# Mixing weights computed in place, a new order in front of the loop, and six of eight roundings on GpSimd

## The reference, cut to what matters

```
# layer 0
y   = grouped_conv1d(x, weight, taps=9, groups=4) + (cond @ c_weight.T)[:, :, None] + bias
w_q = round(weight / w_scale);  y_q = round(y / y_scale)          # int8, a scale for each row
x   = x + float16((y_q @ w_q.T) * y_scale * w_scale)
# layer 1
h   = gelu(cond @ W0 + b0);  h = gelu(h @ W1 + b1)
att = softmax(h @ W2 + b2)                                          # [64 samples, 8]
agg_w = einsum('bk,koi->boi', att, mix_weight)                      # a 64x64 mixing matrix for each sample
z   = einsum('boi,bih->boh', agg_w, x) + (att @ bias_k)[:, :, None]
H   = z @ W.T + b
x   = x + H + ((z @ A) * p_mix) @ Bmat * scaling                    # p_mix: a gate over 8 experts
```

## Time and profile before

| | us |
|---|---|
| median of 3 runs | 638.8 (638.51 to 639.07) |
| the profiled execution, its own time | 637.74 |
| its span, from the first to the last instruction | 635.9 |
| TensorE busy | 609.9 (96%) |
| VectorE / ScalarE / GpSimd busy | 416.4 / 344.6 / 360.4 |
| start of `conv(3)`, the first instruction of the loop on TensorE | 45.98 |

### The profile page before, as it was taken

One profiled execution on the slowest core, in us unless ns is written; L12 is line 12 of the kernel. 1 busy time (PEld: TensorE's weight loads), 2 busy tenths in 40 slices (PEclk: granted clock), 3 DMA queues, 4 the chain that ended last, 5 costly groups with the idle time before them and its releaser, 6 DMA issues.

```text
span 635.9 us, 15749 instructions
## 1 busy us (share of the span) xinstructions
PE 609.9 (96%) x6278; PEld 344.9 (54%) x6311; DVE 416.4 (65%) x849; ACT 344.6 (54%) x608; POOL 360.4 (57%) x242
## 2 busy tenths in 40 slices
PE   8779899999999999999999999999999999999997
PEld 5546566667766666665554444444444444444443
DVE  5968788988788888888258877655444443444434
ACT  2849899888888888876523363423333322332100
POOL 3014545556666666655286978667756667756400
PEclk9799999999999999999999999999999999999999
DMA  9979988788888898865153306974555343441103
GB/s 305 369 154 345 344 308 306 248 307 298 306 320 305 307 322 307 302 216 184 68 187 148 133 31 233 308 292 133 198 199 196 133 166 125 175 132 68 66 2 132
DMA packets 46710, 137.91 MB, mean 217 GB/s; under 512 B 13308, under 2 KB 13596, under 8 KB 46465
## 3 DMA queue, kind: packets, MB, share of 16 engines
q1 hardware_dynamic: 41886, 120.13, 54.5%
q10 hardware_dynamic: 4752, 16.78, 7.0%
HBM read 88.61 MB, written 48.28 MB: 215 GB/s over the span
## 4 chain that ended last, share of the span: by engine, by line
PE 77%; DVE 5%; issue 1%; ACT 1%; DVEq 0%; ACTq 0%
PE ps L885 37%; PE ps L619 12%; PE ps L694 9%; PE ps L524 7%; PE ps L657 3%; PE ps L603 2%; PE ps L867 2%; DVE yb L1414 2%; PE ps L588 2%; PE ps L631 0%; PE ps L662 0%; PE ps L627 0%; ACT yv L992 0%; PE ps L677 0%; DVE yb L1713 0%
## 5 line engine op out<-in xcount | busy, mean ns | idle before, releaser
L1243 POOL TENSOR_TENSOR x<-x_in,f_all 128x512 f32<-128x512 f32 x64 | 74.1, 1160 | 89.2 <-DVE f_all L1449 88.5
L619 PE MATMUL ps<-wqT,yq_both 128*128 128x512 bf16 x479 | 113.2, 379 | 6.5 <-issue 3.7
L1247 POOL TENSOR_TENSOR x_split<-x_ph,x_split 128x1032 f16<-128x1032 f32 x25 | 53.7, 2148 | 64.5 <-ACT x_split L965 64.5
L992 ACT ACTIVATE yv<-yb,yinv 128x128 f32<-128x128 f32 x256 | 77.9, 387 | 2.9 <-DVE yinv L1440 2.9
L619 PEld LDWEIGHTS ps<-wqT,yq_both 128*128 128x128 bf16 x512 | 45.3, 97 | 49.6 <-issue 2.0
L1282 POOL TENSOR_TENSOR ring<-ring 128x512 f32<-128x512 f32 x52 | 66.0, 1269 | 4.0
L694 PE MATMUL ps<-ffn_wT,ring 128*128 128x512 f16 x288 | 64.7, 379 | 0.0
L1449 DVE SCALAR_TENSOR_TENSOR f_all<-ps,tok_scale,wsc_b 128x512 f16<-128x512 f32 x64 | 47.9, 749 | 23.4 <-PE ps L619 22.7
L524 PE MATMUL ps<-x_split,conv_h 128*64 128x256 f16 (+1 forms) x1248 | 59.9, 274 | 1.2 <-POOL conv_h L1297 0.7
L1027 ACT ACTIVATE ring<-ring,pair_inv 128x1024 f32<-128x1024 f32 x26 | 28.4, 1140 | 53.9 <-DVE x_ph L1771 14.4
L524 PEld LDWEIGHTS ps<-x_split,conv_h 128*64 128x64 f16 (+1 forms) x1248 | 48.6, 108 | 9.9 <-issue 6.4
(11 more groups left out here) (338 smaller groups left out, 1203.8 us busy)
## 6 DMA issues: line engine op xcount, KB each, us to landing
x_in<-in_x SPq DMA_DIRECT2D x32, 512.0 KB, 5.8
x_scratch<-x SPq DMA_DIRECT2D x32, 512.0 KB, 3.3
x_ph<-in_x_phases SPq DMA_DIRECT2D x31, 516.0 KB, 4.7
x_scratch<-ring SPq DMA_DIRECT2D x26, 512.0 KB, 4.5
ring<-x_scratch SPq DMA_DIRECT2D x26, 512.0 KB, 4.3
x_in<-x_scratch SPq DMA_DIRECT2D x12, 512.0 KB, 4.4
out<-x_in ACTq DMA_DIRECT2D x12, 512.0 KB, 3.9
wst<-in_w_rows SPq DMA_DIRECT2D x10, 512.0 KB, 6.5
```

The lines of the kernel that those rows point to most:

```text
L619: last = mm(acc_bank(t, h), yqT[:, t % 2, p, :], wqT[:, p, h * HALF:(h + 1) * HALF], start=p == 0, stop=p == PH - 1)
L992: last = A(yv[:, s, :], yb[:, t % 2, s, :], ACT.Copy, scale=yinv[:, s:s + 1], bias=MAGIC)
L1243: g.tensor_tensor(x1[:, t % 2, s], x_in[:, t % 3, s], f16[:, s], ALU.add).then_inc(sem("x1_ready"), 1)
L1247: g.tensor_tensor(x_split[:, (t - SPLIT) % 2, 1, :], phases(t), x_split[:, (t - SPLIT) % 2, 0, :], ALU.subtract).then_inc(sem("xl_ready"), 1)
```

## The change

The program has four parts to it.

1. **Mixing weights in place.** The host lays the mixing weights out a second time, as `mix_rows` [128, 1024]: 128 rows that stand for (output channel within a set of eight, expert, half), and eight blocks of 128 columns, block diagonal in the half. TensorE spreads `att` over the same 128 rows with one matmul (`att_rep` by `pair_of`), VectorE masks it to `att_sets` [128, 32 tiles x 8] (`attention_sets`), and `agg_weights(j)`, called twice, makes four matmuls of 128 rows by 256 columns each. Their result has the input channel on the partition already, so `agg_out` writes `mixT` directly, now without the zero blocks (32 tiles x 64 columns). The two writes to memory, the four reads, the four loads of the old layout and the two zeroings go; one load of 512 KB comes.
2. **New order in front of the loop.** `agg_weights(0)` comes after `wq_transposed(1)`, `agg_weights(1)` ahead of `conv(1)`, `conv(2)` ahead of `wq_transposed(7)`. `warm(12)` is left out. TensorE does `int_product(1, 0)` in front of the loop, so that step 3 has only `int_product(1, 1)`. `small_scales` and its matmul move into step 3, behind `conv_bias(3)`. ScalarE's `scale_rows(2)` moves from the front part into step 3, ahead of `high`, and `tokens_sb(2)` ahead of `row_sums(0)` and the two `z_w` copies. `rank_weights` moves from the end of step 3 to step 4, ahead of `conv_bias(4)`.
3. **Order in steps 4 and 5.** ScalarE copies `z_col` (needed by `rank_pair(0)`) at the start of step 5 and no longer at its end. GpSimd computes the low part of `conv_h` at the start of its pass 4 and no longer behind `add_layer0(3, 1)`.
4. **Six roundings on GpSimd.** `wq_round(2)` to `wq_round(7)` are the same instruction, issued by GpSimd.

```diff
+POOL_ROUNDS, VECTOR_ROUNDS = tuple(range(2, NL)), (0, 1)
...
-        kw = [ring_flat[32 * g:32 * g + NK, 2 * L:3 * L] for g in range(4)]
+        kw = ring[:, 2, :]
...
-        mixT = sb("mixT", [P, NT, P], F32)
-        mix_flat = mixT[:, :, :].rearrange("p a t -> p (a t)").bitcast(F16)
+        mix_home = sb("mix_home", [P, 4 * L], F32)
+        mixT = mix_home[:, 0:NT * CH].rearrange("p (t o) -> p t o", t=NT)
+        mix_flat = mix_home[:, :].bitcast(F16)
         zT = sb("zT", [P, NTOK], F32)
-        agg = zT[:, 0:CH * 32].rearrange("b (i o) -> b i o", i=CH)
...
+            sp.dma_start(kw, mix_rows).then_inc(sem("kw_loaded"), 16)
+            load_wq(3)
             load_phases(1)
-            load_wq(3)
-            for g in range(4):
-                sp.dma_start(kw[g].rearrange("k (h n) -> k h n", h=2),
-                             mix_w.rearrange("k (h g o) i a -> g k h (o i a)", h=2, g=4)[g]).then_inc(sem("kw_loaded"), 16)
...
-            sp.wait_ge(sem("agg_ready"), 4)
-            for h in range(2):
-                sp.dma_start(agg_dram[h], agg[h * B:(h + 1) * B]).then_inc(sem("scratch_saved"), 16)
-            sp.wait_ge(sem("scratch_saved"), 32)
-            sp.wait_ge(sem("zeros_ready"), 3)
-            for h in range(2):
-                for e in range(2):
-                    sp.dma_start(mixT[e * CH:(e + 1) * CH, :, e * CH + 32 * h:e * CH + 32 * h + 32],
-                                 agg_dram[h].rearrange("(t e) i o -> e i t o", e=2)[e]).then_inc(sem("mixT_loaded"), 16)
...
-                pe.wait_ge(sem("wq_rounded"), o + 1)
+                if o in POOL_ROUNDS:
+                    pe.wait_ge(sem("wq_rounded_pool"), POOL_ROUNDS.index(o) + 1)
+                else:
+                    pe.wait_ge(sem("wq_rounded"), VECTOR_ROUNDS.index(o) + 1)
...
-                if o == 3:
-                    pe.wait_ge(sem("agg_ready"), 2)
...
-            def agg_weights():
-                pe.wait_ge(sem("attT_ready"), 1)
-                pe.wait_ge(sem("kw_loaded"), 64)
-                pe.wait_ge(sem("wqT_ready"), 3)
-                for h in range(2):
-                    for g in range(4):
-                        last = mm(agg_bank(g)[h * B:(h + 1) * B, :], attT[32 * g:32 * g + NK, :], kw[g][:, h * 512:(h + 1) * 512], start=True, stop=True)
-                        if h:
-                            last.then_inc(sem("agg_psum"), 1)
+            def agg_weights(j):
+                if j == 0:
+                    pe.wait_ge(sem("att_logits_ready"), 4)
+                    pe.wait_ge(sem("kw_loaded"), 16)
+                wait(pe, "agg_ready", 2 * j)
+                for n in range(4 * j, 4 * j + 4):
+                    o = n % 2 * 8 * NT
+                    last = mm(agg_bank(n // 2)[:, o:o + 8 * NT], kw[:, n * P:(n + 1) * P], att_sets.rearrange("p t s -> p (t s)"), start=True, stop=True)
+                last.then_inc(sem("agg_psum"), 1)
...
-                    pe.wait_ge(sem("mixT_loaded"), 64)
+                    pe.wait_ge(sem("agg_ready"), 4)
...
-                            last = mm(bank(2 + e)[j * 64:(j + 1) * 64, k * CH:(k + 1) * CH], x1[b, t % 2, l:l + 64], mixT[b, t, b],
+                            last = mm(bank(2 + e)[j * 64:(j + 1) * 64, k * CH:(k + 1) * CH], x1[b, t % 2, l:l + 64], mixT[b, t, :],
...
             conv(0)
+            pe.wait_ge(sem("att_logits_ready"), 3)
+            mm(bank(3)[:, 0:NT], att_rep[:, :, :, :].rearrange("b s k e -> b (s k e)"), pair_of[:, :], start=True, stop=True).then_inc(sem("mlp_psum"), 1)
+            tr(bank(2)[0:NK, 192:192 + B], att_n[:, :], ident[0:B, 0:B]).then_inc(sem("mlp_psum"), 1)
             wq_transposed(0)
-            pe.wait_ge(sem("att_logits_ready"), 3)
-            tr(bank(2)[:, 192:192 + B], att4[:, :, :].rearrange("b g k -> b (g k)"), ident[0:B, 0:B]).then_inc(sem("mlp_psum"), 1)
             wq_transposed(1)
-            warm(12)
+            agg_weights(0)
+            pe.wait_ge(sem("pack2_loaded"), 16)
+            pe.wait_ge(sem("attT_ready"), 1)
+            mm(bank(2)[0:B, 256:256 + CH], attT[:, :], pk[0:NK, PACK["mixb"]], start=True, stop=True).then_inc(sem("mlp_psum"), 1)
+            tr(bank(2)[0:R, 384:384 + E], pk[0:E, PACK["limes"]], ident[0:E, 0:E]).then_inc(sem("mlp_psum"), 1)
             max_rows(0)
             wq_transposed(2)
             max_back(0)
+            agg_weights(1)
             conv(1)
-            agg_weights()
-            pe.wait_ge(sem("pack2_loaded"), 16)
-            mm(bank(2)[0:B, 256:256 + CH], attT[0:NK, :], pk[0:NK, PACK["mixb"]], start=True, stop=True).then_inc(sem("mlp_psum"), 1)
-            tr(bank(2)[0:R, 384:384 + E], pk[0:E, PACK["limes"]], ident[0:E, 0:E]).then_inc(sem("mlp_psum"), 1)
+            wq_transposed(3)
+            wq_transposed(4)
+            wq_transposed(5)
+            tokens_out(0)
+            wq_scales_out(0)
             max_rows(1)
-            wq_transposed(3)
-            tokens_out(0)
-            wq_transposed(4)
+            int_product(0, 0)
             max_back(1)
-            wq_transposed(5)
-            wq_scales_out(0)
-            int_product(0, 0)
             wq_transposed(6)
+            conv(2)
             wq_transposed(7)
             wq_scales_out(1)
+            tokens_out(1)
+            int_product(0, 1)
+            pe.wait_ge(sem("yinv_ready"), 2)
+            max_rows(2)
+            int_product(1, 0)
+            max_back(2)
             pe.wait_ge(sem("s_max_ready"), 9)
-            pe.wait_ge(sem("yinv_ready"), 2)
             tr(ps_small[0:9, 160:288], s_max[:, :], ident[:, :]).then_inc(sem("s_top_psum"), 1)
-            conv(2)
-            pe.wait_ge(sem("s_top_ready"), 1)
-            mm(ps_small[:, 300:309], s_top[:, 0:1].to_broadcast([9, P]), ident[0:9, 0:9], start=True, stop=True).then_inc(sem("s_top_psum"), 1)
-            int_product(0, 1)
-            tokens_out(1)
-            pe.wait_ge(sem("s_scale_ready"), 1)
-            max_rows(2)
-            max_back(2)
...
+                if c == 3:
+                    pe.wait_ge(sem("s_top_ready"), 1)
+                    pe.wait_ge(sem("yinv_ready"), 3)
+                    mm(ps_small[:, 300:309], s_top[:, 0:1].to_broadcast([9, P]), ident[0:9, 0:9], start=True, stop=True).then_inc(sem("s_top_psum"), 1)
...
-                int_product(c - 2, 0, 0, 4)
-                if SPLIT <= c + LEAD < NT:
+                if c > 3:
+                    int_product(c - 2, 0, 0, 4)
...
+                    int_product(c - 2, 0, 4, 8)
+                int_product(c - 2, 1, 0, 3)
+                if c == 3:
+                    pe.wait_ge(sem("s_scale_ready"), 1)
                     x_total(c + LEAD)
-                for n in range(2):
...
-                A(agg[:, :, 8 * j:8 * j + 8].rearrange("b i o -> b o i"),
-                  agg_bank(j).rearrange("b (o i) -> b o i", o=8), ACT.Copy).then_inc(sem("agg_ready"), 1)
+                act.wait_ge(sem("agg_psum"), j // 2 + 1)
+                A(mixT[:, :, 16 * j:16 * j + 16].rearrange("p t (n s) -> p t n s", n=2), agg_bank(j).rearrange("p (n t s) -> p t n s", n=2, s=8), ACT.Copy).then_inc(sem("agg_ready"), 1)
...
+            act.wait_ge(sem("mlp_psum"), 5)
+            A(attT[:, :], bank(2)[0:NK, 192:192 + B], ACT.Copy).then_inc(sem("attT_ready"), 1)
             wq_out(0)
-            act.wait_ge(sem("mlp_psum"), 4)
-            A(attT[:, :], bank(2)[:, 192:192 + B], ACT.Copy).then_inc(sem("attT_ready"), 1)
             wq_out(1)
-            wq_out(2)
-            scale_rows(0)
             agg_out(0)
             agg_out(1)
+            wq_out(2)
             agg_out(2)
             agg_out(3)
-            act.wait_ge(sem("mlp_psum"), 5)
-            act.wait_ge(sem("mlp_psum"), 6)
+            act.wait_ge(sem("mlp_psum"), 7)
             A(agg_b[:, :], bank(2)[0:B, 256:256 + CH], ACT.Copy).then_inc(sem("agg_b_ready"), 1)
             act.wait_ge(sem("gate_w_ready"), 1)
             A(gate_w[0:R, E:2 * E], bank(2)[0:R, 384:384 + E], ACT.Copy).then_inc(sem("limesT_ready"), 1)
+            scale_rows(0)
             wq_out(3)
+            wq_out(4)
             tokens_sb(0)
-            wq_out(4)
+            wsc_out(0)
             wq_out(5)
-            wsc_out(0)
+            wq_out(6)
             scale_rows(1)
-            wq_out(6)
             wq_out(7)
             wsc_out(1)
-
             tokens_sb(1)
-            scale_rows(2)
-            act.wait_ge(sem("s_scale_ready"), 2)
-            act.wait_ge(sem("zeros_ready"), 1)
...
+                if c == 5:
+                    act.wait_ge(sem("z_col_psum"), 1)
+                    A(z_col[64:ZW, :], bank(7)[64:ZW, 0:1], ACT.Copy).then_inc(sem("z_col_ready"), 1)
...
+                scale_rows(c - 1)
                 if c == 3:
+                    high(0, 0)
+                    high(0, 1)
+                    act.wait_ge(sem("s_scale_ready"), 2)
```

(74 more changed lines are left out.)

56 lines of the change are left out of this document (28 added, 28 removed).

## The result

The changed kernel took 633.27 us (median of 4, 630.61 to 634.21), the kernel before 638.88 us (median of 4, 638.51 to 639.07): a ratio of 0.990 with a 95% interval of 0.988 to 0.993, 5.6 us less. I had forecast 635.2 us, with 633.7 to 637.8 as the range. The direction held; the size fell out of the range at its lower end.

The account below looks back on a forecast made before the run. TensorE was busy 609.9 of 635.9 us, but ScalarE was taken to set the time around 104 us. On its path 3.2 - 1.4 + 1.8 = 3.6 us, so 638.8 - 3.6 = 635.2 us, range 633.7 to 637.8.

Parts of the forecast that it names:

- The trip through memory: Before the loop: its reads land by about 43 us, `mix(0)` starts at 48.78, so removal alone gains nothing.
- New mixing weights: In front of the loop: 1.8 us per `agg_weights` call, 0.6 per `agg_out` copy, 0.4 for `attention_sets`.
- Rounding on GpSimd: In front of the loop: 1.1 us each, hidden up to 2.2 us; VectorE loses 4.5 us of work.
- The front part: From the end of `conv(0)` to `conv(3)`: `conv(3)` at 42.8 us, 3.2 us earlier.
- Step 3: After `conv(3)`: a new TensorE gap of about 1.55 us; `conv(4)` loses 0.8 us, ScalarE 1.4 us.
- Steps 5 and 6: TensorE's waits of 0.98 and 0.74 us go; ScalarE no longer idles 1.72 us and sets the pace.
- The sum on the profiled execution: Whole kernel: 3.6 us less on ScalarE's path, from 637.74 to 634.1 us.
- Against the median: Whole kernel: the same 3.6 us taken off the median of 638.8, giving 635.2 us.
- (b): Whole kernel, shorter still: no hand-over losses, no low clock, 4.1 or up to 5 us gained; 633.6 to 634.2, chance 0.11.
- (c): Front part: new waits between ScalarE and TensorE cost 1.4 to 2.2 us more; 636.5 to 637.5, chance 0.10.
- (d): Roundings slow or held by VectorE, or one clock fall in step 3's new gap; 637.6 to 639.8, chance 0.10.
- (e): Clock falls in step 3's gap, staying low through `conv(4)` and step 4: slower, up to 641.7 us, chance 0.06.

Follow-up runs that it names:

- a_trip: The changed kernel with the mixing weights' trip through memory added back, written in runs of 128 bytes, new order kept: 640.84 us, ratio 1.003 to the kernel before.
- a_round_dve: The changed kernel with all eight roundings on VectorE, each behind its inverse: 632.88 us, ratio 0.990 to the kernel before.
- a_again: The changed kernel measured again without an edit: 633.31 us, ratio 0.992 to the kernel before.
- b_fill25: The kernel before with 24 idle matmuls of 128 columns in TensorE's gap of 1.72 us before `max_rows(1)`: 640.13 us, ratio 1.003.
- a_zbias2: The changed kernel with ScalarE's `z_bias` scaling only two columns, the others left unscaled: 633.08 us, ratio 0.991 to the kernel before.
- b_again: The kernel before measured again without an edit: 637.89 us, ratio 0.9996.
- b_gate: The kernel before with the eighth gate's transpose moved four blocks of matmuls later, filling the gap near 345 us: 634.74 us, ratio 0.994.
- a_int3: The changed kernel with `int_product(1, 0)` and `layer0(1, 0)` put back into step 3: 634.27 us, ratio 0.993 to the kernel before.
- a_fill: The changed kernel with ScalarE's `row_sums(0)` and two `z_w` copies of step 3 ahead of `tokens_sb(2)`: 633.69 us, ratio 0.993 to the kernel before.
- a_gate: The changed kernel with the eighth gate's transpose moved four blocks of matmuls later: 629.54 us, ratio 0.986 to the kernel before.

## Why the prediction was wrong, step by step

**What bounds the kernel.** Right. What came earlier at `split_conv(9)` came earlier at the end: the rest was 536.93 and 536.90 us in the two first profiles. That nothing after it waits for a clock was wrong in a part of the executions, because of the fall near 345 us, which the one profile of before did not have.

**The trip through memory, worth nothing by itself.** For the profiled execution this holds: the earlier trace rows show the reads landed well before `mix(0)`. As a rule it was wrong. The prediction noted that the loop's first loads stood behind the trip in SP's queue and that no row shows an engine waiting for them; that is true of the one profile with the longest opening. In the six other profiles of the old order ScalarE waits 0.38 to 3.48 us for the third of these loads. In the new order no profile shows such a wait, except a_trip with a trip put back (2.62 us), which lost 7.5 us, part of it by its own small runs. That the trip is what holds the loads is read from the queue's times; no run takes the trip alone away.

**New mixing weights.** Each call of `agg_weights` took 1.95 to 1.99 us (1.8 forecast), an `agg_out` copy 0.59 (0.6), `attention_sets` 0.41 (0.4).

**Rounding on GpSimd.** 1.12 us, forecast 1.1. The cost was right; my reading that VectorE's 4.5 us fewer are part of what makes the front shorter was wrong (a_round_dve). During a rounding VectorE's reductions and small scales ran at their usual lengths, so of the mutual exclusion weighed in the prediction, from "SBUF — State Buffer", "Who interferes with whom", of the Trainium skill, no loss is seen here. It was hardly put to the test: few small scales overlap a rounding.

**The front part.** 3.2 us forecast, 3.2 in the first profile and 3.45 in a_again. `conv(3)` stands 27.1 us after the end of `conv(0)`, forecast 27.15. That it came so close is in part luck: TensorE was busy for 24.0 us of it, forecast 25.0, and waited 3.1, forecast 2.15. b_fill25 adds that the fall of the clock was worth at most some 0.7 us there; the rest goes by the order of work. Of its parts only the roundings were taken back alone (a_round_dve), so which of the others gives how much stays open.

**Step 3.** A new gap of 1.30 us (1.55 forecast), and `conv(4)` 5.58 us after the end of `conv(3)` (5.95). ScalarE's `phase_high(6)` came 9.2 us after the end of `conv(3)` (51.78 less 42.61), before 8.3: 0.9 us lost, where I had charged 1.4. This is the largest single part of the difference between the two sums below.

**Steps 5 and 6.** Both waits went, and ScalarE set the pace from step 6 to step 9 without a gap, as a_zbias2 confirms. From `conv(3)` to `split_conv(9)` it came to 0.74 us less, where my terms (1.8 gained, 1.4 lost) made 0.4.

**The sum on the profiled execution** was 0.8 us too small: 3.6 us against the 4.4 us of two executions with nearly the same opening. Of this 0.25 us lie in the front part, 0.34 in the steps, and 0.2 in an opening and a rest that were a little shorter in a_again and have nothing to do with the change.

**Against the median: this step failed.** I wrote that the profiled execution's "own time is 1.06 under the median; against the median 638.8 - 3.6 = 635.2 us", and so carried the 1.06 us over to the changed kernel as if it were a constant. It is not one. After a like opening the changed kernel's profiled execution took 633.33 us and its median is 633.31: the 1.06 us had become nothing. So the forecast of 635.2 was 1.9 us above what was measured, 1.06 by this step and 0.8 by the sum. What the 1.06 us are in the kernel before is only known in part. The second profile of it, b_again, took 638.17 us with an opening 1.3 us shorter, and its loss against the first lies near 345 us, where the clock fell; b_gate, without the gap there, is 1.05 us lower than the gap explains. Both speak for that fall. How many executions have it can't be read from the times and mean clocks, so this stays open, and so does what the waits for the loop's loads add. What the new order did remove is the fall in front of the loop: of its nine executions without an edit seven had a mean granted clock of 1.000, and of the 93 of the kernel before that were measured beside the experiments none had more than 0.997. With the sum made against the profiled execution, and nothing added, the forecast had been 634.1 us, inside its own rival (b) and still 0.8 us above the measured time.

**The rivals.** (b) came nearest, with the low clock nowhere and up to 5 us; the measured 5.6 us (5.0 in a_again) lie at or beyond its end, and at 0.11 it had too little. Neither (c) nor (d) came about. (e), a fall in step 3's new gap, was seen in no profile of the new order with its gap of 1.30 us; in a_trip the clock fell there, with a gap of 2.89 us. The old order's pair of gaps before `conv(3)` had a fall in two profiles of seven. The fall that (d) and (e) priced at 6.65 us is 6.8 us by the clock's row, which changes neither.

## What to carry to other kernels

A profile is one execution: before its sum is carried to a median, take a second profile of the kernel before and see which gaps are followed by a fall of the clock in one and not in the other. Where TensorE sets the pace such a gap is worth closing for its own length and for the half-rate microseconds that can follow; moving one small transpose behind work that needs nothing from it gave 3.1 to 3.7 us, over half of what this whole change did. Where another engine sets the pace, closing one gave nothing (a_int3, a_fill). A gain at the start of a kernel arrives only if what stands behind it can come earlier too: look for gaps in which the clock can fall, and for loads that stand in a queue behind a transfer whose time does not move.

## What the runs showed of the hardware

- **The first 15 us run at either rate.** Before and after the change, and with nothing changed, `conv(0)` took 2.98 us or between 3.9 and 4.8 us, and the two small groups of float32 matmuls before it ran at full or at half rate. In six profiles with a long `conv(0)` (a_gate among them) the granted clock shows a fall of 3.4 us there. In the eight others it stood at 1.00, as in a_again, although `conv(0)` took up to 4.79 us; in these the durations and not the clock row tell. A dozen more matmuls of 128 columns ahead of the first load made it 2.98 us in all five profiles.
- **The same gap is followed by a fall or not.** With 2.65 us without TensorE near 345 us the granted clock went to 1.2 GHz for 3.4 us in six profiles and stayed at 2.4 GHz in nine. One such fall stretched 15 matmuls from 3.40 to 4.95 us.
- **A fall costs little where other engines set the time.** The one at 25 us, 6.8 us at 1.2 GHz by the clock's row, cost the kernel before at most 0.74 us.
- **Small runs hold the queue.** Two writes from SBUF to memory in runs of 128 bytes held SP's queue for 10.50 us in a_trip, 0.63 for the first and 9.82 for the second; two writes of the same 0.5 MB each in whole rows took 1.16 us together.
- **Loads behind a trip through memory keep their time.** With openings from 12.62 to 15.72 us the loop's first load was issued at 42.6 to 43.9 us in all seven profiles of the old order, and ScalarE waited 0.38 to 3.48 us for the third one in six of them.
